# Third layer's attentions: two of four heads turned by VectorE and DMA instead of TensorE

## Chip, cores, metric

One of the cores of one Trainium2 chip. The time is device microseconds of a whole run of the program, which computes four layers one after another; lower is better.

## The reference

Four cross-attention layers follow each other on x (8, 256, 512). The change lies in the third one, which has a self attention, a cross attention and an MLP. Its attentions are, cut to what matters:

```python
NH = 16; HD = 32
def attention(q, k, v, mask):
    scores = jnp.einsum('bhqd,bhkd->bhqk', q, k) / jnp.sqrt(jnp.float32(HD))
    scores = scores * mask - 10000.0 * (1.0 - mask)
    probs = jax.nn.softmax(scores, axis=-1)
    return jnp.einsum('bhqk,bhkd->bhqd', probs, v)
ln_out = layernorm(hidden_states, ln1_s, ln1_b)
q, k, v = jnp.split(ln_out @ w_qkv + b_qkv, 3, axis=-1)
x = hidden_states + merge_heads(attention(..., ltor_mask)) @ w_ao + b_ao
q = layernorm(x, ln2_s, ln2_b) @ w_q + b_q
k, v = jnp.split(encoder_states @ w_kv + b_kv, 2, axis=-1)
x = x + merge_heads(attention(..., cross_mask)) @ w_co + b_co
```

Here hidden_states and encoder_states are (8, 256, 512): 8 batch elements, 256 rows, 16 heads of 32.

## The kernel before

`program` calls `l0_attention`, `l1_layer`, `l2_attentions` and `l2_mlp` in turn. `l2_attentions` goes through 16 **slots**: the self attention of the 8 batch elements (slots 0 to 7), then the cross attention of the 8 (slots 8 to 15). A slot has four **steps** (off 0 to 3), and a step k handles four heads ("quad"), so there are K = 64 steps. The order of the work on each engine is written out by hand in a loop over k; engines meet at semaphores. PSUM banks 0 to 3 hold the scores of the four heads, banks 4 to 7 are a ring: each label in `ring` takes the next of the four and waits until the one four before it is drained.

In step k each engine does, in this order:

- TensorE: `turn_probs(k-1, i)` for four heads (four 128x128 transposes each, L2297), the first half of a product for a neighbour slot (k, v and q for the next slot in off 0, 1, 2, the output projection p of the last slot in off 3; 24 matmuls of 256 columns or 12 of 512 in three passes hi/lo, L2363 and L2367), `turn_sums(k-1)` (L2306), `scores(k+1)` (L2286), `weigh_values(k-1)` (probabilities times values, L2321), then the second half of the product and, where a slot needs it, the turning of normalised x or of u (`turn_in`, L2384): in off 3 for self slots, in off 1 (x) and off 3 (u) for cross slots.
- ScalarE: `probs(k-1, i)` copies the turned probabilities of each head out of PSUM (L2421), `exponentials(k, i)` (L2414), the bias of k or q, copies of sums and outputs, the high half of what was turned in (T_hi), the store of x3.
- VectorE: the normalised rows xn (L931), `maxima(k, i)` (L2530, two per head), `low_outputs(k-2)` (L2548), the first half of v or p (L2565, L2568), `mask(k+1)` (scores out of PSUM times the mask, L2523, one per head), `outputs(k-1)` (values' sum times the reciprocal, L2543), T_lo (the low half of what was turned in, L2589, before which the next product can't start), the statistics of a row (L912), `reciprocals(k)`, the second half of v or p.
- GpSimd: the sums' reciprocals copied to rows, the standard deviations, the bias added to x (L2270).
- SP: all loads of the stage, each behind the wait it needs. It stands outside the loop over k.

The masked scores lie in `sc`, three of them in rotation; the probabilities are written in place, and turned into `probT`, two in rotation.

The first layer (`l0_attention`) turns its probabilities in another way: ScalarE writes them in runs of 32 (L566), VectorE transposes blocks of 32x32 (STREAM_TRANSPOSE, L797), and `move` (L281) brings the blocks to their partitions by 16 DMAs per half, issued by SP and GpSimd; its value matmuls read the result in runs of 32 elements.

## Time and profile before

| | |
|---|---|
| time, median of 3 runs | 3328.47 us (3325.46 to 3334.11) |
| profiled execution | 3319.85 us |
| its span | 3317.2 us |
| granted TensorE clock, mean | 0.963 |
| busy: PE, PEld, DVE, ACT, POOL | 93%, 72%, 71%, 53%, 21% |
| third layer's attentions | about 2130 to 2866 us of the span |

In the rows of a trace, PE is TensorE, DVE VectorE, ACT ScalarE, POOL GpSimd, SPq, ACTq and POOLq the queues that issue DMAs. Names like l2a_bank<-l2a_T_hi,l2a_w_hi_q are output and inputs by the program's names; L2363 is a line of the kernel. A bracket at the end of a row of a timeline is the idle time before it and who ended it.

### The profile page before, as it was taken

To read this page: it belongs to the slowest core of one execution; us is meant where nothing else is said; L and a number is where in the kernel's file an instruction comes from. 1 tells how busy PE (TensorE), PEld (TensorE's weight loads), DVE (VectorE), ACT (ScalarE), POOL (GpSimd) and SP (SyncE) were. 2 spreads that over 40 slices of the span, in tenths; PEclk is the share of its full clock that TensorE was granted. 3 is DMA by queue.
4 is the path that set the end of the run, shared out by engine and by line. 5 is a ranking of instruction groups with operands and counts; after the bars stand their busy time and mean duration, and the time that the engine had idled before them with its cause. 6 is when DMAs were issued, how large, how long until landed. Compare 5 with 4: busy or idle time off the path is not lost. (4 is left out here: it accounts for less than half of the span.)

```text
span 3317.2 us, 55559 instructions
## 1 busy us (share of the span) xinstructions
PE 3087.4 (93%) x20384; PEld 2377.3 (72%) x20384; DVE 2357.7 (71%) x3589; ACT 1742.7 (53%) x4185; POOL 698.2 (21%) x1206
## 2 busy tenths in 40 slices
PE   7999999999999977899999996689999999799999
PEld 6778788878878845566666663478887788587777
DVE  5777767777667656999999998167777878642321
ACT  4555445545454534465555643257787777532222
POOL 2554544545444430000000000011101111000000
PEclk9999999999999988899999998789999999899999
DMA  7779776877676664454455543300011111211000
GB/s 250 235 236 283 237 208 193 244 228 214 204 222 198 191 212 109 109 121 112 111 119 114 116 107 81 121 1 14 27 62 55 46 46 43 100 71 39 32 15 18
DMA packets 175325, 426.40 MB, mean 129 GB/s; under 512 B 52656, under 2 KB 60848, under 8 KB 150608
## 3 DMA queue, kind: packets, MB, share of 16 engines
q1 hardware_dynamic: 115936, 232.42, 25.3%
q10 hardware_dynamic: 28272, 127.46, 10.8%
q0 software_dynamic: 30848, 62.97, 7.6%
q8 instruction: 164, 2.69, 0.3%
q14 instruction: 105, 0.86, 0.1%
HBM read 229.76 MB, written 58.72 MB: 87 GB/s over the span
## 5 line engine op out<-in xcount | busy, mean ns | idle before, releaser
L281 POOL DMA_DIRECT2D l_probT<-l_prob x896 | 441.4, 500 | 253.7 <-DVE l_prob L797 234.3
L775 DVE TENSOR_REDUCE l_nmax<-l_bank 128x1 f32<-128x512 f32 x512 | 316.6, 680 | 182.3 <-PE l_bank L443 182.2
L566 ACT ACTIVATE l_prob<-l_bank,l_nmax 128x512 f32<-128x512 f32 x512 | 344.9, 689 | 132.8 <-DVE l_nmax L775 123.9
L797 DVE STREAM_TRANSPOSE l_prob<-l_prob 128x1024 f32<-128x1024 f32 x256 | 314.1, 1228 | 23.2 <-ACT l_prob L566 9.7
L409 PE MATMUL l_bank<-l_x_hi,l_w_hi 128*128 128x256 f32 x1024 | 298.3, 291 | 21.7 <-DVE l_x_lo L866 11.6
L409 PE MATMUL l_bank<-l_x_hi,l_w_lo 128*128 128x256 f32 x1024 | 291.4, 285 | 0.0
L409 PE MATMUL l_bank<-l_x_lo,l_w_hi 128*128 128x256 f32 x1024 | 291.0, 284 | 0.0
L1836 DVE TENSOR_TENSOR_SCAN l_kv<-l_wx,l_kv 128x2056 f32<-128x2056 f32 x64 | 283.8, 4434 | 3.1 <-DVE l_sxc L1957 1.5
L2414 ACT ACTIVATE l2a_sc<-l2a_sc,l2a_nmax 128x256 f32<-128x256 f32 x512 | 254.7, 508 | 41.0 <-DVE l2a_nmax L2530 41.0
L468 PE MATMUL l_bank<-l_probT,l_v 128*64 128x256 f32 x2048 | 241.4, 388 | 12.7 <-issue 6.8
L409 PEld LDWEIGHTS l_bank<-l_x_hi,l_w_hi 128*128 128x128 f32 x1024 | 197.6, 193 | 45.3 <-issue 37.4
L468 PEld LDWEIGHTS l_bank<-l_probT,l_v 128*64 128x64 f32 x2048 | 143.6, 139 | 104.8 <-issue 32.9
L2530 DVE CUSTOM_DVE_ANT_0 l2a_sc<-l2a_sc,l2a_mb 128x256 f32<-128x256 f32 x512 | 217.0, 483 | 0.0
L409 PEld LDWEIGHTS l_bank<-l_x_hi,l_w_lo 128*128 128x128 f32 x1024 | 198.0, 193 | 0.0
L409 PEld LDWEIGHTS l_bank<-l_x_lo,l_w_hi 128*128 128x128 f32 x1024 | 197.9, 193 | 0.0
L2523 DVE SCALAR_TENSOR_TENSOR l2a_sc<-l2a_bank,l2a_m 128x512 f32<-128x512 f32 x256 | 158.6, 680 | 54.2 <-PE l2a_bank L2286 54.2
L3069 DVE TENSOR_TENSOR l2b_h_lo<-l2b_hf,l2b_h_hi 128x512 fp32r<-128x512 f32 x64 | 44.2, 691 | 198.5 <-ACT l2b_h_hi L2975 198.3
L370 POOL TENSOR_TENSOR l_oT<-l_oT,l_rT 128x512 f32<-128x512 f32 x64 | 96.5, 1507 | 367.7 <-ACT l_oT L602 367.7
L1828 DVE TENSOR_TENSOR l_kv<-l_vb,l_ik 128x2048 f32<-128x2048 f32 x64 | 145.8, 2278 | 7.5 <-DMA l_vb<-vd 7.1
L427 PE MATMUL l_bank<-l_wv_hi,l_x_hi 128*128 128x256 f32 x512 | 148.3, 290 | 2.1 <-DVE l_wv_lo L834 2.1
L2297 PE MATMUL l2a_bank<-l2a_ident,l2a_sc 128*128 128x128 f32 x1024 | 133.2, 277 | 16.6 <-DVE l2a_oT L2543 8.7
L1844 DVE TENSOR_TENSOR l_kv<-l_kv,l_ir 128x2048 f32<-128x2048 f32 x64 | 146.1, 2284 | 0.1
(360 smaller groups left out, 7890.0 us busy)
## 6 DMA issues: line engine op xcount, KB each, us to landing
l_probT<-l_prob SPq DMA_DIRECT2D x1152, 64.0 KB, 2.9
l_vb<-vd SPq DMA_DIRECT2D x64, 1024.0 KB
l_probT<-l_prob POOLq DMA_DIRECT2D x896, 64.0 KB, 2.5
l_w_hi<-kept_w_hi ACTq DMA_DIRECT2D x24, 1024.0 KB, 5.7
l_w_lo<-kept_w_lo ACTq DMA_DIRECT2D x24, 1024.0 KB, 5.7
l_wv_hi<-kept_wv_hi ACTq DMA_DIRECT2D x12, 1024.0 KB, 8.3
l_wv_lo<-kept_wv_lo ACTq DMA_DIRECT2D x12, 1024.0 KB, 10.2
l2a_x<-x SPq DMA_DIRECT2D x16, 512.0 KB, 3.6
```

Source lines behind the costliest of these rows:

```text
L281: eng.dma_start(probT[i % RING][r * SQ:(r + 1) * SQ, g, :, :, :, :], prob[i % RING][g * SQ:(g + 1) * SQ, r * IT:(r + 1) * IT, :, :, :]).th ...
L409: mm = pe.matmul(s.ap[:, c * ROWS:(c + 1) * ROWS], a[:, kt, c, g, :], b[:, kt, c * ROWS:(c + 1) * ROWS], start=m == 0, stop=m == 3 * KT - 1)
L427: mm = pe.matmul(s.ap[:, at], a[:, kt, jt * P:(jt + 1) * P], b[:, kt, c, :, :], start=m == 0, stop=m == 3 * KT - 1)
L468: mm = pe.matmul(s.ap[own, f * ROWS:(f + 1) * ROWS], v[l][:, pair % 2, j, own], half[:, :, :, j, h, :], start=j == 0, stop=j == IT - 1)
L566: act.activation(prob[i % RING][:, :, it % 2, h, :].rearrange("p (q t) s -> p t q s", q=Q), s.ap[:, :].rearrange("p (t q s) -> p t q s", t ...
L775: dve.tensor_reduce(nmax[:, n % 2, it, h:h + 1], s.ap[:, :], AX.X, ALU.max, negate=True).then_inc(max_ready, 1)
L797: dve.transpose(own, own).then_inc(turned, 1)
L1836: dve.tensor_tensor_scan(own, wx[:, :, :].rearrange("p j t -> p (j t)"), own, 0.0, ALU.mult, ALU.add)\
L1844: dve.tensor_tensor(own, own, ir[:, ct, :].unsqueeze(1).to_broadcast([P, NJ, ROWS]), ALU.mult).then_inc(z_ready, 1)
L2414: ins = act.activation(to[:, r, :], to[:, r, :], ACT.Exp, scale=-1.0, bias=nmax[:, k % SC_RING, i, r:r + 1], accum_out=rsum[:, k % SC_RING ...
L2523: dve.scalar_tensor_tensor(out=sc[k % SC_RING][i][:, :, :], in0=s.ap[:, :].rearrange("p (r j) -> p r j", r=RT), scalar=HD ** -0.5, in1=own ...
L2530: dve.tensor_tensor_reduce(out=to[:, r, :], in0=to[:, r, :], in1=own[:, r, :], scale=-1.0, scalar=3.0e38, op0=ALU.add, op1=ALU.min, accum_ ...
```

## The change

Heads 0 and 1 of each quad no longer pass through TensorE. ScalarE writes their probabilities to a new buffer `prob` in runs of 32; `turn_blocks(k)` on VectorE transposes it in blocks of 32x32 (128x1024 elements) back into the place in `sc`; `move_heads(k)` moves the blocks to their partitions by 16 DMAs of 32 partitions x 256 elements (32 KB), 8 issued by SP and 8 by GpSimd, into `turned_by_dma` (two in rotation). `weigh_values` waits for them (`heads_moved`), and so does `mask` three steps later. Heads 2 and 3 go on as before. The ring has 2 labels fewer a step. On VectorE `turn_blocks(k)` stands before the masks of k+1, and `outputs(k-1)` stands between the masks of heads 0 and 1 and those of heads 2 and 3. On ScalarE `exponentials(k, 1)` comes ahead of the first half of the product. On GpSimd the moves stand after the bias and ahead of the deviations. On SP the loads are now taken in the loop over k, each behind the moves of its step.

```diff
--- before.py
+++ after.py
@@ -2036,7 +2036,7 @@
     return plan
 
 
-def l2_attentions(nc, kept_rows, rows_in, d, x2, u, mask_self, mask_cross, x3):
+def l2_attentions(nc, kept, kept_rows, rows_in, d, x2, u, mask_self, mask_cross, x3):
 
     SLOTS = [(b, a) for a in range(2) for b in range(B)]
     NS = len(SLOTS)
@@ -2046,6 +2046,10 @@
     XB = 4
     Q4 = range(QUAD)
     SC_RING, V_RING = 3, 2
+    BY_DMA, BY_PE = range(2), range(2, QUAD)
+    SQ, Q = 32, 4
+    MOVES = [(g, q) for g in range(Q) for q in range(Q)]
+    BY_SP = 8
     WEIGHTS = ["k0", "v0", "q0", "o0", "k1", "v1", "q1", "o1"]
     SPLIT_AT = {-5: "k0", -4: "v0", -3: "q0", -2: "o0", 25: "k1", 27: "v1", 28: "q1", 37: "o1"}
     NORMED = {"k0": 0, "v0": 0, "q0": 0, "q1": 1}
@@ -2092,7 +2096,7 @@
     ring = []
     for k in range(FIRST, LAST):
         quad = 0 <= k - 1 < K
-        ring += [f"t{k - 1}_{i}" for i in Q4] if quad else []
+        ring += [f"t{k - 1}_{i}" for i in BY_PE] if quad else []
         ring += ["b" + BIAS_AT[k]] if k in BIAS_AT else []
         what, z = product_of(k)
         ring += [f"{what}{z}_0"] if what else []
@@ -2123,10 +2127,18 @@
         scs = [ph.sb(f"sc{n}", [P, QUAD, RT, ROWS]) for n in range(SC_RING)]
         sc = [[s[:, i, :, :] for i in Q4] for s in scs]
         raw_sc = [s[:, :, :, :].rearrange("p i r n -> p (i r n)").rearrange("p (c n) -> p c n", c=CT) for s in scs]
-        probT = [[ph.sb(f"probT{n}{i}", [P, RT, ROWS]) for i in Q4] for n in range(2)]
+        probT = [{i: ph.sb(f"probT{n}{i}", [P, RT, ROWS]) for i in BY_PE} for n in range(2)]
+        turned_by_dma = [ph.sb(f"turned{n}", [P, Q, 2, RT, RT, SQ]) for n in range(2)]
+        blocks = [s[:, 0:2, :, :].rearrange("p i r n -> p (i r n)") for s in scs]
+        by_quarter = [a.rearrange("p (q e) -> p q e", q=Q) for a in blocks]
+        prob = ph.sb("prob", [P, Q * 2 * 2 * RT * SQ])
+        by_head = prob[:, :].rearrange("p (q i m s) -> p i m q s", q=Q, i=2, m=2 * RT)
         oT = [ph.sb(f"oT{i}", [P, ROWS]) for i in range(2)]
         oT_hi, oT_lo = [[ph.sb(f"oT_{part_}{i}", [P, CT, ROWS], F32R) for i in range(2)] for part_ in ("hi", "lo")]
         m, mb = [[ph.sb(f"{name}{i}", [P, RT, ROWS]) for i in range(2)] for name in ("m", "mb")]
+        turned_blocks = ph.sem("turned_blocks")
+        moved_sp = [ph.sem(f"moved_sp{n}") for n in range(2)]
+        moved_pool = [kept.enter_context(nc.semaphore(f"kept_moved_heads{n}")) for n in range(2)]
         nmax, rsum = ph.sb("nmax", [P, SC_RING, QUAD, RT]), ph.sb("rsum", [P, SC_RING, QUAD, RT])
         rinv = ph.sb("rinv", [P, 2, QUAD, RT])
         rows = ph.sb("rows", [P, RT, QUAD, HD])
@@ -2160,6 +2172,20 @@
         def drained(eng, s):
 
             eng.wait_ge(s.drained, s.k + 1)
+
+        def heads_moved(eng, k):
+
+            eng.wait_ge(moved_sp[k % 2], 16 * BY_SP * (k // 2 + 1))
+            eng.wait_ge(moved_pool[k % 2], 16 * (len(MOVES) - BY_SP) * (k // 2 + 1))
+
+        def move_heads(eng, k, pieces, moved):
+
+            eng.wait_ge(turned_blocks, k + 1)
+            if k >= 2:
+                full(eng, S[f"o{k - 2}"])
+            for g, q in pieces:
+                eng.dma_start(turned_by_dma[k % 2][q * SQ:(q + 1) * SQ, g, :, :, :, :].rearrange("p i r t s -> p (i r t s)"),
+                              by_quarter[k % SC_RING][g * SQ:(g + 1) * SQ, q, :]).then_inc(moved[k % 2], 16)
 
         def norm_count(z):
 
@@ -2227,20 +2253,17 @@
                     load_b(n)
                 load_m(0)
                 load_w("k1", "k0")
-                for z in range(4, B):
-                    load_x(z)
-                load_u(B)
-                load_x(B)
-                load_w("v1", "k1")
-                load_w("q1", "v1")
-                load_x(B + 1)
-                load_u(B + 1)
-                load_w("o1", "q1")
-                load_m(1)
-                for b in range(2, B):
-                    load_x(B + b)
-                    load_u(B + b)
-                    load_m(b)
+                for k in range(K):
+                    move_heads(sp, k, MOVES[:BY_SP], moved_sp)
+                    s, off = k // GROUPS, k % GROUPS
+                    if off == 0 and XB <= s + 2 < NS:
+                        load_x(s + 2)
+                    if k == 4 * B - 9 or off == 1 and B < s + 2 < NS:
+                        load_u(B if s + 2 < B else s + 2)
+                    if off == 3 and 0 < s - 6 < B:
+                        load_m(s - 6)
+                    if k in (25, 27, 29):
+                        load_w({25: "v1", 27: "q1", 29: "o1"}[k], {25: "k1", 27: "v1", 29: "q1"}[k])
                 sp.wait_ge(w_lo_ready, len(WEIGHTS))
                 for l in range(LANES):
                     sp.wait_ge(stored[l], 16 * (B // XB + 1))
@@ -2260,8 +2283,6 @@
                         pool.tensor_copy(rows[:, :, :, :], rinv[:, (k - 1) % 2, :, :].rearrange("p i r -> p r i").unsqueeze(3)
                                          .to_broadcast([P, RT, QUAD, HD])).then_inc(rows_ready, 1)
                     what, z = norm_of(k)
-                    if what == "stats":
-                        deviations(pool, mv, sd, eps, power, norm_count(z) - 1, 0, var_signal, sd_ready)
                     if what == "rows":
                         a = SLOTS[z][1]
                         pool.wait_ge(xn_ready, norm_count(z))
@@ -2269,6 +2290,10 @@
                         to = x[z % XB]
                         pool.tensor_tensor(to[:, :, :], to[:, :, :], brow[f"o{a}"][:, :].unsqueeze(1).to_broadcast([P, RT, COLS]),
                                            ALU.add).then_inc(xb_ready, 1)
+                    if 0 <= k < K:
+                        move_heads(pool, k, MOVES[BY_SP:], moved_pool)
+                    if what == "stats":
+                        deviations(pool, mv, sd, eps, power, norm_count(z) - 1, 0, var_signal, sd_ready)
 
             @block.tensor
             def _(pe):
@@ -2313,13 +2338,18 @@
                     if g == 0:
                         for half in range(2):
                             drained(pe, S[f"v{z}_{half}"])
-                    for i in Q4:
+                    for i in BY_PE:
                         drained(pe, S[f"t{k}_{i}"])
+                    heads_moved(pe, k)
                     for j in range(RT):
                         for i in Q4:
                             h = g * QUAD + i
+                            if i in BY_PE:
+                                prob = probT[k % 2][i][:, j, :]
+                            else:
+                                prob = turned_by_dma[k % 2][:, :, i, :, j, :].rearrange("p g r s -> p r g s")
                             mm = pe.matmul(s.ap[HD * i:HD * i + HD, 0:ROWS], v[z % V_RING][:, j, h * HD:(h + 1) * HD],
-                                           probT[k % 2][i][:, j, :], start=j == 0, stop=j == RT - 1)
+                                           prob, start=j == 0, stop=j == RT - 1)
                     mm.then_inc(s.full, 1)
 
                 def bias(n):
@@ -2387,7 +2417,7 @@
                 pe.wait_ge(consts, 2)
                 for k in range(FIRST, LAST):
                     if 0 <= k - 1 < K:
-                        for i in Q4:
+                        for i in BY_PE:
                             turn_probs(k - 1, i)
                     if k in BIAS_AT:
                         bias(BIAS_AT[k])
@@ -2409,9 +2439,13 @@
             def _(act):
                 def exponentials(k, i):
                     act.wait_ge(max_ready, RT * (k * QUAD + i + 1))
-                    to = sc[k % SC_RING][i]
+                    if i == 0 and k:
+                        act.wait_ge(turned_blocks, k)
                     for r in range(RT):
-                        ins = act.activation(to[:, r, :], to[:, r, :], ACT.Exp, scale=-1.0, bias=nmax[:, k % SC_RING, i, r:r + 1],
+                        own = to = sc[k % SC_RING][i][:, r, :]
+                        if i in BY_DMA:
+                            own, to = own.rearrange("p (t q s) -> p t q s", t=RT, q=Q), by_head[:, i, RT * r:RT * r + RT, :, :]
+                        ins = act.activation(to, own, ACT.Exp, scale=-1.0, bias=nmax[:, k % SC_RING, i, r:r + 1],
                                              accum_out=rsum[:, k % SC_RING, i, r:r + 1])
                     ins.then_inc(exp_ready, 1)
 
@@ -2486,15 +2520,15 @@
                 act.wait_ge(vec_in, 16)
                 for k in range(FIRST, LAST + 2):
                     if 0 <= k - 1 < K:
-                        for i in Q4:
+                        for i in BY_PE:
                             probs(k - 1, i)
                     if 0 <= k < K:
                         exponentials(k, 0)
+                        exponentials(k, 1)
                     product(k, 0)
                     if 0 <= k - 1 < K:
                         sums(k - 1)
                     if 0 <= k < K:
-                        exponentials(k, 1)
                         exponentials(k, 2)
                     if not turned_last(k):
                         turned(k)
@@ -2513,11 +2547,13 @@
 
             @block.vector
             def _(dve):
-                def mask(k):
+                def mask(k, heads):
                     own = m[mask_of(*SLOTS[k // GROUPS])]
                     if k == 0:
                         dve.wait_ge(w_lo_ready, WEIGHTS.index("o0") + 1)
-                    for i in Q4:
+                    if k >= SC_RING and heads == BY_DMA:
+                        heads_moved(dve, k - SC_RING)
+                    for i in heads:
                         s = S[f"s{k}_{i}"]
                         full(dve, s)
                         dve.scalar_tensor_tensor(out=sc[k % SC_RING][i][:, :, :], in0=s.ap[:, :].rearrange("p (r j) -> p r j", r=RT),
@@ -2529,6 +2565,10 @@
                     for r in range(RT):
                         dve.tensor_tensor_reduce(out=to[:, r, :], in0=to[:, r, :], in1=own[:, r, :], scale=-1.0, scalar=3.0e38,
                                                  op0=ALU.add, op1=ALU.min, accum_out=nmax[:, k % SC_RING, i, r:r + 1]).then_inc(max_ready, 1)
+
+                def turn_blocks(k):
+                    dve.wait_ge(exp_ready, QUAD * k + len(BY_DMA))
+                    dve.transpose(blocks[k % SC_RING], prob[:, :]).then_inc(turned_blocks, 1)
 
                 def reciprocals(k):
                     dve.wait_ge(exp_ready, QUAD * (k + 1))
@@ -2634,12 +2674,16 @@
                         bias(BIAS_AT[k])
                     if not (0 <= k < K and product_of(k)[0] == "p"):
                         product(k, 0)
+                    if 0 <= k < K:
+                        turn_blocks(k)
                     if 0 <= k + 1 < K:
                         if (k + 1) % GROUPS == 0 and SLOTS[(k + 1) // GROUPS][1] == 1:
                             dve.wait_ge(mb2_ready, SLOTS[(k + 1) // GROUPS][0] + 1)
-                        mask(k + 1)
+                        mask(k + 1, BY_DMA)
                     if 0 <= k - 1 < K:
                         outputs(k - 1)
+                    if 0 <= k + 1 < K:
+                        mask(k + 1, BY_PE)
                     if turned_last(k):
                         product(k, 1)
                     turned(k)
@@ -3167,7 +3211,7 @@
         between_layers.close()
         kept_rows = kept.enter_context(nc.sbuf_tensor("kept_rows", [P, CT, COLS], F32))
         rows_in = [kept.enter_context(nc.semaphore(f"kept_rows_in{l}")) for l in range(LANES)]
-        l2_attentions(nc, kept_rows, rows_in, d, x2, u, d["mask_self"], d["mask_cross"], x3)
+        l2_attentions(nc, kept, kept_rows, rows_in, d, x2, u, d["mask_self"], d["mask_cross"], x3)
         l2_mlp(nc, kept_rows, rows_in, d, x3, u, out)
 
 
```

## Rows read from the trace of the kernel before

**Rows 1.** Stretches: span, busy us (instructions) of five engines, clock, DMA share, GB/s; self and cross slot.

```profile
2290.00:2331.35 41.35, 40.90 (x355) 33.30 (x354) 32.63 (x105) 31.35 (x98) 5.05 (x7) 1.00 0.07 27
2638.20:2680.80 42.60, 41.70 (x362) 34.14 (x361) 34.12 (x109) 32.23 (x101) 5.16 (x7) 1.00 0.13 44
```

**Rows 2.** Timeline of SP's queue (start, us until the last ends, what, count): loads of x.

```profile
2283.31 124.39 SPq L2191 DMA_DIRECT2D l2a_x<-x  x4
```

**Rows 3.** Timeline of VectorE in a cross slot (start, us, what, count, idle before).

```profile
2624.42 1.06 DVE L931 TENSOR_SCALAR l2a_xn<-l2a_x,l2a_mv,l2a_sd 128x512 f32<-128x512 f32 x2 [1.01 <-POOL l2a_sd L925]
...
2635.07 1.29 DVE L2589 TENSOR_TENSOR l2a_T_lo<-l2a_bank,l2a_T_hi 128x512 fp32r<-128x512 f32 x2 [0.37 <-ACT l2a_T_hi L2468]
...
2649.82 0.69 DVE L2568 TENSOR_TENSOR l2a_x<-l2a_bank,l2a_x 128x512 f32<-128x512 f32 x1 [3.82 <-PE l2a_bank L2367]
...
2661.63 2.48 DVE L2523 SCALAR_TENSOR_TENSOR l2a_sc<-l2a_bank,l2a_m 128x512 f32<-128x512 f32 x4 [1.73 <-PE l2a_bank L2286]
...
2667.02 1.05 DVE L931 TENSOR_SCALAR l2a_xn<-l2a_x,l2a_mv,l2a_sd 128x512 f32<-128x512 f32 x2 [1.01 <-POOL l2a_sd L925]
```

**Rows 4.** Timeline of TensorE in the same cross slot: end of the wait for T_lo, q0, transposes.

```profile
2635.81 1.25 PE L2297 MATMUL l2a_bank<-l2a_ident,l2a_sc 128*128 128x128 f32 x8 [0.41 <-DVE l2a_T_lo L2589]
2636.82 0.36 PE L2363 MATMUL l2a_bank<-l2a_T_hi,l2a_w_hi_q 128*128 128x256 f32 x1
...
2644.97 1.91 PE L2297 MATMUL l2a_bank<-l2a_ident,l2a_sc 128*128 128x128 f32 x16
2646.63 0.51 PE L2367 MATMUL l2a_bank<-l2a_w_hi_o,l2a_oT_hi 128*128 128x512 f32 x1
```

**Rows 5.** Timeline of VectorE and TensorE in a self slot: T_lo, k0, v0, v1, masks.

```profile
2310.93 1.27 DVE L2589 TENSOR_TENSOR l2a_T_lo<-l2a_bank,l2a_T_hi 128x512 fp32r<-128x512 f32 x2
...
2313.33 0.36 PE L2363 MATMUL l2a_bank<-l2a_T_hi,l2a_w_hi_k 128*128 128x256 f32 x1
...
2326.29 0.69 DVE L2565 TENSOR_TENSOR l2a_v<-l2a_bank,l2a_b_v 128x512 f32<-128x512 f32 x1 [2.39 <-PE l2a_bank L2367]
...
2331.44 0.69 DVE L2565 TENSOR_TENSOR l2a_v<-l2a_bank,l2a_b_v 128x512 f32<-128x512 f32 x1 [1.05 <-PE l2a_bank L2367]
...
2337.20 2.48 DVE L2523 SCALAR_TENSOR_TENSOR l2a_sc<-l2a_bank,l2a_m 128x512 f32<-128x512 f32 x4 [1.97 <-PE l2a_bank L2286]
```

**Rows 6.** Groups by line, 2200 to 2490: the transposes on TensorE (busy us, mean ns, idle before).

```profile
L2297 PE MATMUL l2a_bank<-l2a_ident,l2a_sc 128*128 128x128 f32 x448 | 58.0, 279 | 6.7 <-DVE l2a_oT L2543 5.3 <-ACT l2a_rT L2428 1.4
```

**Rows 7.** First layer: transpose (ns min/median/max), one step's moves (timeline), landing (page, part 6).

```profile
L797 DVE STREAM_TRANSPOSE l_prob<-l_prob x256: 1187/1236/1247, 35.6 to 1196.4; 128x1024 f32<-128x1024 f32 x128
...
601.19 5.87 SPq L281 DMA_DIRECT2D l_probT<-l_prob  x9
...
601.46 3.46 POOL L281 DMA_DIRECT2D l_probT<-l_prob  x7 [0.73 <-DVE l_prob L797]
...
l_probT<-l_prob SPq DMA_DIRECT2D x1152, 64.0 KB, 2.9
```

**Rows 8.** Stretches with a gap on TensorE, and one stretch after it (columns as in rows 1).

```profile
390.00:393.00 3.00, 0.39 (x2) 0.00 (x0) 1.75 (x3) 0.00 (x0) 0.00 (x0) 1.00 1.06 242
393.00:397.00 4.00, 3.29 (x18) 2.17 (x20) 1.72 (x3) 2.79 (x8) 0.00 (x0) 0.57 0.85 245
...
1491.00:1494.00 3.00, 0.88 (x4) 0.48 (x3) 2.35 (x3) 3.00 (x5) 0.00 (x0) 1.00 0.53 131
...
2221.00:2226.00 5.00, 1.22 (x10) 0.74 (x7) 5.00 (x19) 4.48 (x16) 0.20 (x1) 1.00 0.00 0
2226.00:2233.00 7.00, 6.32 (x31) 6.32 (x32) 5.18 (x22) 4.34 (x13) 0.49 (x1) 0.52 0.00 0
```

**Rows 9.** Timeline of VectorE in the last slot: masks two steps apart, the last outputs.

```profile
2829.13 2.47 DVE L2523 SCALAR_TENSOR_TENSOR l2a_sc<-l2a_bank,l2a_m 128x512 f32<-128x512 f32 x4
...
2842.08 2.47 DVE L2523 SCALAR_TENSOR_TENSOR l2a_sc<-l2a_bank,l2a_m 128x512 f32<-128x512 f32 x4
...
2857.04 0.42 DVE L2543 TENSOR_TENSOR l2a_oT<-l2a_bank,l2a_rT 128x256 f32<-128x256 f32 x1 [2.75 <-PE l2a_bank L2321]
```

## The prediction

> **What bounds the kernel now.** I read the busy time of each engine in stretches first. In the third layer's attentions TensorE is busy for 40.9 of the 41.35 us that one slot of four steps takes in the self half, and 41.7 of 42.6 in the cross half; VectorE is at 32.6 and 34.1 [rows 1]. The pitch of a slot is read twice: four loads of x in 124.39 us, so 41.34 each [rows 2], and two normalisations 42.60 apart in the cross half [rows 3]. So TensorE sets the pace, but VectorE has only 8.5 us of idle per slot, and the timelines show where both meet. Two places matter. In cross slots VectorE ends T_lo (the low half of the turned x, off 1) at 2636.3; TensorE starts q0 at 2636.82, and VectorE gets p0 of the slot before at 2649.82, after 3.82 us of waiting [rows 3, 4]. In self slots T_lo (off 3) ends at 2312.2, TensorE starts k0 at 2313.33, and VectorE gets v0 at 2326.29 and v1 at 2331.44 [rows 5]. These chains across both engines decide what becomes of a lighter TensorE.
>
> **TensorE loses 8 transposes a step.** 16 take 1.91 us from the first start to the last end, 1.66 from their start to that of the product behind them (2644.97 to 2646.63) [rows 4], so two heads cost 0.83 us a step and 3.3 us a slot. The 448 transposes between 2200 and 2490 were 58.0 us busy [rows 6], so they are no small part. ScalarE loses two copies a step; it is not late anywhere in these rows, and I take nothing for it. The value matmuls now read runs of 32 elements and ScalarE writes such runs: the first layer does both all the time; I price both at nothing (a gain is impossible, and if each of the 8 reads took 0.05 us longer, 1.6 us a slot would go into TensorE's slack).
>
> **VectorE gains a transpose of 128x1024 a step.** The same instruction in the first layer takes 1236 ns [rows 7]; from one to the next it is about 1.2, which I take: 4.8 us a slot. By busy time alone the self slot would be VectorE's 32.6 + 4.8 + 1.0 (the wait for the deviations, 1.01 [rows 3]) = 38.4, the cross slot about 40.2. TensorE would be at 37.6 and 38.4. Both engines are then within 2 us of each other, so the chains decide.
>
> **Cross slots.** Chain on TensorE from T_lo's end to p0: 13.0 us now (2636.82 to 2649.82), less 0.83 for one group of two heads, plus 0.1 to start: 12.3. On VectorE from p0 to the next T_lo's end: the pitch 42.60 makes that end 2678.9, so 29.1 us, less the waits for TensorE and ScalarE in it, 1.73 and 0.37 [rows 3], is 27.0. The transposes of off 3, 0 and 1 lie in it and nothing there can hide them, since VectorE runs in order: + 3.6 = 30.6. Sum 42.9, less the 0.1 by which the rows overlap: 42.8, against 42.6 now. The 3.3 us off TensorE are thus not gained: only one of its four groups lies on this chain. 8 such slots (7 to 14): +0.2 each, **+1.6 us**.
>
> **Self slots.** TensorE from T_lo to v0: 12.96 now (2313.33 to 2326.29), less 0.83, plus 0.1: 12.2. From v0 to v1 TensorE needs 5.15 as now; VectorE would need 4.8. From v1 to the next T_lo's end VectorE takes 22.0 now (2331.44 to 2312.2 + 41.34), less 1.97 of waiting [rows 5], plus two transposes: 22.5. Sum 39.9: a gain of 1.5 a slot. Six slots (1 to 6): **-9.0 us**. Slot 0 has no projection, and VectorE waits in it; I take 0.
>
> **The DMAs.** Each step issues 8 on SP and 8 on the Pool queue. In the first layer 9 take SP 5.87 us and 7 take Pool 3.46 [rows 7], so SP needs 5.2 for 8 and Pool 4.0; an issue lands 2.9 us later [rows 7]. Together about 7.5 us from the transpose's end (pieces here have half the bytes, so rather less). I walked each slot with this: the transpose's end lies 8.3 us or more ahead of the value matmuls that need it, so some 0.8 us remain in self slots and 1.4 in cross slots. Cost: nothing, while this cover holds; every us beyond it is a us of TensorE on the chain. On SP, loads now queue behind the moves, and the moves of the next step behind a load that waits for a store: the store goes out at the end of step off 0, the next moves some 5 us later. On Pool the deviations come behind 4.0 us of issues; the statistics end about 4.3 us after the transpose, so sd is about as late as now. The rows copy has more time than that.
>
> **The outputs between the masks.** VectorE scales outputs(k-1) 1.2 us earlier. Now TensorE waits 0.4 to 0.5 us a slot for a bank it frees, and the ring has 6 labels a step in place of 8; no gain is left where VectorE sets the pace. The price of the new order is that masks 2 and 3 stand behind the value matmuls, 1.1 us after the first scores; the masks of heads 0 and 1 (1.2 us) cover it.
>
> **The clock.** With the chains above, TensorE in a cross slot ends the transposes of off 1 and then waits for T_lo: its work since the last chain point ends 3.7 us before. In the trace of before, such gaps are followed by a granted clock of half (1.2 instead of 2.4 GHz): after 2.6 of 3 us idle from 390 and after 3.8 of 5 from 2221, where the next 7 us ran at 0.52 [rows 8]. Of 18 gaps of more than 2.5 us that began at full clock between 60 and 2230 (those are the first and the last), 17 were followed by a fall; a gap of 2.12 (from 1491) was not [rows 8], and those near 2 us went either way. Four us at a mean of 0.57 (from 393) are 3.4 at half [rows 8]; so a fall costs 1.7 us of TensorE's work. In cross slots it falls on q0, on the chain: 8 x 1.7 = **+13.6**. In self slots the idle is 0.65 and 2.3 us with 0.85 of work between; I take a fall in half of six slots: **+5.1**. Bounds: 0 (the gaps don't lower it) and 3.4 a slot (a fall of 7 us, as after 2226).
>
> **The last slot and the end.** Slot 15 has no products but p; a step takes 6.5 us now (2829.13 to 2842.08 for two) [rows 9]. Two steps of the new loop are: moves 7.5, value matmuls and outputs 1.7, masks, maxima, transpose 5.7: 14.9, so 7.4 a step: 4 x 0.9 = **+3.6**. At the end the last value matmuls now end at 2857.0 [rows 9]; in the new kernel they wait for the last moves. The last transpose ends at about 2852.7, + 7.5 + 1.1 = 2861.3: **+4.3**, and the gap before it (4 us) makes the last projection run at half clock: **+1.7**.
>
> **Sum.** -9.0 + 1.6 + 13.6 + 5.1 + 3.6 + 4.3 + 1.7 = +20.9 us. The profiled execution took 3319.85 us (span 3317.2), so it would be 3340.8; the median of the runs is 8.6 us above it, so 3328.5 + 20.9 = **3349.4**. A measurement of this kernel can tell about 0.3% (10 us) from no change.
>
> A page of the Trainium skill speaks for the change: "VectorE: DVE Perf Modes", section "The three transpose paths", gives a 128x128 block of bf16 390 ns on TensorE and 311 on VectorE. The rows here (fp32, in streams) have 0.104 us a block on TensorE and 0.15 on VectorE, so the measured order is the reverse; by the page's ratio the transposes would cost VectorE 0.66 us a step and the cross chain would be 1.6 us shorter.
>
> **Rivals.**
> 1. *The clock holds.* Same chains, no falls: -9.0 + 1.6 + 3.6 + 4.3 = +0.5, **3329.0**. For it: gaps near 2 us went either way. Against: 17 of 18 above 2.5.
> 2. *The waits fill.* If the engines run further ahead of each other than my walk lets them, only busy time counts: self 38.4 (-3.0 x 6), cross 40.2 (-2.4 x 8), end +7.9: -29.3, **3299**. For it: VectorE waits 3.82 for p0 and TensorE never waits long now. Against: p0 stands in VectorE's order before the transposes that it would have to run ahead of.
> 3. *The moves are late* (slower still, and what decides against the change even without the clock). If they take 10 us from the transpose, 2.5 more than above, TensorE stands 1.7 longer in self and 1.1 in cross slots, twice in self: 6 x 3.4 + 8 x 1.1 = +29 beyond the forecast, **3378**. It starts to count from 8.3 us. For it: SP issues at 0.65 each, and one move is late if any is. Against: pieces are half as big, and the DMA share is 0.07 to 0.13 here [rows 1]. The skill's "SBUF — State Buffer", section "SBUF: two separate sides", says that Pool can't write descriptors while VectorE holds the shared port in a fast mode; by it xn (1.06 us) could hold Pool up by that much once a slot. The first layer's Pool issues [rows 7] show none.
>
> **Chances.** Forecast 0.44, clock holds 0.22, waits fill 0.24, moves late 0.10. Faster than 0.3%: the third and a little of the second, 0.26. Within: most of the second, a little of the first, 0.22. Slower: 0.52. The range that keeps 8 in 10 goes from 3298 (half of the fill case is left out) to 3372; the forecast's own is 3335 to 3362, its clock term between 0 and twice.
>
> **What would show it.** VectorE at 38 to 40 us busy a slot, with a wait for p0 of about 3 us left in cross slots; a cross pitch of 42.8 without falls and 44.5 with; a self pitch of 39.9 to 41.6; TensorE waiting for T_lo 2 to 4 us a slot; the granted clock under 1.00 in windows of cross slots; the value matmuls hardly waiting for the moves. Wrong if the cross pitch is under 42 (chain), if the clock stays 1.00 with gaps over 2.5 us, or if the value matmuls wait for a DMA for more than 1 us.

## Result and the profile after

The changed kernel takes 3335.8 us (median, 3329.4 to 3347.1), beside 3327.2 for the kernel before on the same chips: ratio 1.0028, 95% interval 1.0018 to 1.0037. So it is 9 us slower where 20.9 were forecast: the direction holds, the size is less than half. The interval lies clear of 1, but the loss is no larger than the 10 us that the prediction took as the least that can be told. The profiled execution took 3333.0 us (span 3331.2).

The page of the changed kernel, busy time and the DMAs (part 1, two lines of part 5 and two of part 6):

```profile
PE 3056.0 (92%) x19872; PEld 2338.6 (70%) x19872; DVE 2430.5 (73%) x3653; ACT 1681.4 (50%) x4057; POOL 951.5 (29%) x1718
...
L2187 POOL DMA_DIRECT2D l2a_turned<-l2a_sc x512 | 251.8, 499 | 317.4 <-DVE l2a_sc L2571 286.5
...
L2559 DVE SCALAR_TENSOR_TENSOR l2a_sc<-l2a_bank,l2a_m 128x512 f32<-128x512 f32 x256 | 161.4, 668 | 18.1 <-DMA l2a_turned<-l2a_sc 13.0
...
l2a_turned<-l2a_sc SPq DMA_DIRECT2D x512, 32.0 KB, 2.0
l2a_turned<-l2a_sc POOLq DMA_DIRECT2D x512, 32.0 KB, 1.8
```

A move takes GpSimd 0.50 us to issue and lands 1.8 to 2.0 us later. The 13.0 us for which the masks (L2559) seem to wait for a move are really waits for late scores: they come right after a fall of the clock (at 2635.50, say, 0.1 us after the scores end, when the move in question had long landed), and in e1, without the falls, they are gone from the cross slots. By the ends of T_lo on VectorE (one in each self slot, in off 3; two in each cross slot, in off 3 and off 1) the stage falls into stretches. All times are us from one profiled execution each:

| stretch | before | after | difference |
|---|---|---|---|
| six self slots (2187.6 to 2436.0 before) | 248.4 | 242.1 | -6.3 |
| change from self to cross (to 2507.5) | 71.5 | 65.3 | -6.2 |
| seven cross slots (to 2806.7) | 299.3 | 306.9 | +7.6 |
| last T_lo to last p | 57.7 | 70.2 | +12.6 |
| stage, first T_lo to the next stage's first instruction | 730.1 | 738.0 | +7.9 |

The expectations below still have 306.3, 70.8 and 13.2 for the changed kernel; they take the end of its last T_lo 0.6 us too early.

The rest of the profiled difference (3.8 ahead of the stage, 2.3 behind it) lies in code that is the same. The stretches answer to [rows 1]: one self slot, one cross slot with a fall of the clock, the change between the halves, the stretch with five cross slots, and the part of it right after a T_lo (columns as there):

```profile
2313.43:2353.20 39.77, 37.70 (x321) 29.80 (x320) 37.27 (x110) 27.25 (x90) 20.65 (x40) 1.00 0.29 81
2690.00:2734.00 44.00, 40.19 (x330) 32.34 (x329) 38.42 (x113) 28.51 (x92) 20.84 (x39) 0.96 0.31 91
2433.60:2498.90 65.30, 63.23 (x517) 51.65 (x516) 61.92 (x171) 47.52 (x143) 31.52 (x58) 0.95 0.40 123
...
2590.00:2810.00 220.00, 201.14 (x1640) 161.14 (x1639) 195.88 (x577) 144.57 (x468) 104.23 (x195) 0.96 0.30 87
2629.40:2632.80 3.40, 3.26 (x15) 3.29 (x16) 3.40 (x19) 2.22 (x9) 0.48 (x1) 0.50 0.62 180
```

In the self slot VectorE is busy for 37.3 us beside TensorE's 37.7: both ran up to the same level, as the sum had it (38.4 and 37.6), and a slot still takes 2.1 us more than either. The cross slot's clock is 0.96. VectorE's timeline where a cross slot turns x answers to [rows 3] (start, us, what, count, idle before):

```profile
2623.67 1.23 DVE L2571 STREAM_TRANSPOSE l2a_sc<-l2a_prob 128x1024 f32<-128x1024 f32 x1
...
2626.00 0.40 DVE L2583 TENSOR_TENSOR l2a_oT<-l2a_bank,l2a_rT 128x256 f32<-128x256 f32 x1
...
2627.53 0.67 DVE L2605 TENSOR_TENSOR l2a_v<-l2a_bank,l2a_b_v 128x512 f32<-128x512 f32 x1
2628.13 1.26 DVE L2629 TENSOR_TENSOR l2a_T_lo<-l2a_bank,l2a_T_hi 128x512 fp32r<-128x512 f32 x2
...
2643.20 0.69 DVE L2608 TENSOR_TENSOR l2a_x<-l2a_bank,l2a_x 128x512 f32<-128x512 f32 x1 [2.92 <-PE l2a_bank L2397]
```

The transpose (1.23 us) stands ahead of the scaled outputs, v1 and T_lo, and VectorE still waits 2.92 us for p0 (3.82 before). TensorE beside it, to compare with [rows 4]:

```profile
2623.89 1.06 PE L2414 MATMUL l2a_bank<-l2a_ident,l2a_xn 128*128 128x128 f32 x8
2626.46 0.66 PE L2322 MATMUL l2a_bank<-l2a_ident,l2a_sc 128*128 128x128 f32 x4 [1.50 <-DVE l2a_oT L2583]
2628.25 0.66 PE L2322 MATMUL l2a_bank<-l2a_ident,l2a_sc 128*128 128x128 f32 x4 [1.14 <-DVE l2a_v L2605]
2629.54 0.55 PE L2393 MATMUL l2a_bank<-l2a_T_hi,l2a_w_hi_q 128*128 128x256 f32 x1 [0.63 <-DVE l2a_T_lo L2629]
...
2633.93 0.27 PE L2331 MATMUL l2a_bank<-l2a_ident,l2a_rows 128*128 128x128 f32 x1
```

It waits 1.50, 1.14 and 0.63 us within 5 us, each time for the next thing that VectorE finishes, and then runs q0 at a granted clock of half for 3.4 us. In a self slot (compare [rows 5]) only the last wait is as long, and 3 us of a product lie between the second and the third:

```profile
2346.49 0.66 PE L2414 MATMUL l2a_bank<-l2a_ident,l2a_xn 128*128 128x128 f32 x4 [0.26 <-DVE l2a_x L2608]
2347.57 0.50 PE L2397 MATMUL l2a_bank<-l2a_w_hi_o,l2a_oT_hi 128*128 128x512 f32 x1 [0.42 <-ACT l2a_rT L2462]
2350.87 0.66 PE L2322 MATMUL l2a_bank<-l2a_ident,l2a_sc 128*128 128x128 f32 x4 [0.22 <-DVE l2a_oT L2583]
2352.66 0.66 PE L2322 MATMUL l2a_bank<-l2a_ident,l2a_sc 128*128 128x128 f32 x4 [1.14 <-DVE l2a_T_lo L2629]
```

TensorE in the last slot (compare [rows 9]): in the same view of before it waits 0.16 us once for the rows of the reciprocals; it now waits 2.5 to 4.4, then for the last moves, and scores and last projection start at half the clock.

```profile
2828.11 0.41 PE L2331 MATMUL l2a_bank<-l2a_ident,l2a_rows 128*128 128x128 f32 x2 [2.47 <-POOL l2a_rows L2283]
...
2835.88 0.66 PE L2331 MATMUL l2a_bank<-l2a_ident,l2a_rows 128*128 128x128 f32 x2 [3.39 <-POOL l2a_rows L2283]
2836.47 2.09 PE L2311 MATMUL l2a_bank<-l2a_k,l2a_q 32*128 32x256 f32 x16
...
2846.22 0.66 PE L2331 MATMUL l2a_bank<-l2a_ident,l2a_rows 128*128 128x128 f32 x2 [4.37 <-POOL l2a_rows L2283]
...
2863.50 0.41 PE L2331 MATMUL l2a_bank<-l2a_ident,l2a_rows 128*128 128x128 f32 x2 [3.57 <-POOL l2a_rows L2283]
2865.24 0.64 PE L2351 MATMUL l2a_bank<-l2a_turned,l2a_v 128*32 128x256 f32 x2 [1.33 <-DMA l2a_turned<-l2a_sc]
...
2868.72 0.76 PE L2397 MATMUL l2a_bank<-l2a_w_hi_o,l2a_oT_hi 128*128 128x512 f32 x1 [1.54 <-DVE l2a_oT_lo L2588]
```

### The profile page after: what moved, and what is told of

It is laid out like the page before. It is cut to its first block and busy times, and to the rows that moved or that the text cites. A ratio compares the mean times of both kernels' runs of the same rounds, so it can differ in the third digit from the quotient of the medians.

```text
span 3331.2 us, 55617 instructions
## 1 busy us (share of the span) xinstructions
PE 3056.0 (92%) x19872; PEld 2338.6 (70%) x19872; DVE 2430.5 (73%) x3653; ACT 1681.4 (50%) x4057; POOL 951.5 (29%) x1718
## 3 DMA queue, kind: packets, MB, share of 16 engines
q10 hardware_dynamic: 28272, 127.46, 10.8%
## 5 line engine op out<-in xcount | busy, mean ns | idle before, releaser
L2187 POOL DMA_DIRECT2D l2a_turned<-l2a_sc x512 | 251.8, 499 | 317.4 <-DVE l2a_sc L2571 286.5
L409 PE MATMUL l_bank<-l_x_hi,l_w_hi 128*128 128x256 f32 x1024 | 299.0, 292 | 20.8 <-DVE l_x_lo L866 11.3
L2559 DVE SCALAR_TENSOR_TENSOR l2a_sc<-l2a_bank,l2a_m 128x512 f32<-128x512 f32 x256 | 161.4, 668 | 18.1 <-DMA l2a_turned<-l2a_sc 13.0
L2448 ACT ACTIVATE l2a_prob<-l2a_sc,l2a_nmax 128x256 f32<-128x256 f32 x256 | 127.2, 503 | 79.6 <-DVE l2a_nmax L2566 79.1
```

The lines of the kernel that those rows point to most:

```text
L409: mm = pe.matmul(s.ap[:, c * ROWS:(c + 1) * ROWS], a[:, kt, c, g, :], b[:, kt, c * ROWS:(c + 1) * ROWS], start=m == 0, stop=m == 3 * KT - 1)
L2187: eng.dma_start(turned_by_dma[k % 2][q * SQ:(q + 1) * SQ, g, :, :, :, :].rearrange("p i r t s -> p (i r t s)"), by_quarter[k % SC_RING][g ...
L2559: dve.scalar_tensor_tensor(out=sc[k % SC_RING][i][:, :, :], in0=s.ap[:, :].rearrange("p (r j) -> p r j", r=RT), scalar=HD ** -0.5, in1=own ...
```

## Experiments

Every ratio is against the kernel before on the same chip, with its 95% interval; the changed kernel's is 1.0028. The stretches of each profile:

| kernel | self | change | cross | end | ratio |
|---|---|---|---|---|---|
| before | 248.4 | 71.5 | 299.3 | 57.7 | |
| changed | 242.1 | 65.3 | 306.9 | 70.2 | 1.0028 (1.0018 to 1.0037) |
| e1 TensorE kept busy in cross slots | 242.6 | 65.3 | 298.5 | 67.6 | 0.9999 (0.9987 to 1.0011) |
| e2 half of each transpose | 238.8 | 63.8 | 297.5 | 66.5 | 0.9974 (0.9960 to 0.9989) |
| e3 outputs after all masks | 243.4 | 68.7 | 310.0 | 70.7 | 1.0061 (1.0042 to 1.0081) |
| e4 more of ScalarE's time | 242.3 | 66.1 | 306.2 | 71.5 | 1.0036 (1.0022 to 1.0051) |
| e5 self slots only | 242.6 | 67.7 | 299.3 | 57.7 | 0.9975 (0.9960 to 0.9991) |
| e6 self slots and off 2 | 244.8 | 65.2 | 294.7 | 56.8 | 0.9956 (0.9940 to 0.9972) |
| e7 not in the last slot | 243.8 | 65.2 | 308.4 | 59.4 | 0.9999 (0.9985 to 1.0012) |
| e8 all moves on SP | 288.3 | 77.7 | 358.9 | 88.4 | 1.0388 (1.0363 to 1.0413) |
| e9 outputs' place alone | 248.5 | 70.9 | 295.4 | 59.0 | 0.9989 (0.9976 to 1.0002) |
| e10 off 2 and outputs' place | 244.6 | 65.3 | 290.7 | 56.7 | 0.9932 (0.9916 to 0.9947) |
| e11 ScalarE issues at the end | 244.3 | 66.2 | 307.0 | 75.4 | 1.0040 (1.0028 to 1.0052) |
| e12 no GpSimd moves at the end | 242.2 | 65.2 | 306.3 | 69.0 | 1.0027 (1.0015 to 1.0039) |
| e13 TensorE kept busy at the end | 242.6 | 66.0 | 306.3 | 73.1 | 1.0042 (1.0025 to 1.0060) |

A self stretch moves by up to 2.7 us from profile to profile of the same code there (242.1 to 244.8): in e6, e7, e10 and e11 the third self slot has a fall of the clock and takes 41.5 in place of 39.8. A cross stretch moves by 2 with the number of falls.

**e1: is it the clock?** In `turn_probs` and `turn_in`:

```diff
+                    for _ in range({2: 3, 3: 2}[i] if k >= 4 * B and k % GROUPS == 1 else 1):
+                        for _ in range(3 if what == "x" and z > B else 1):
```

> Added to the changed kernel: TensorE repeats transposes that it has just made, with the same data into the same banks, in the cross slots only: those of x three times (off 1), those of heads 2 and 3 at the start of off 2 three times and twice. They lie where TensorE waits for VectorE (1.50, 1.14 and 0.63 us in the slot that starts at 2607), so no chain gets longer. Theory (a gap of 3.3 us with 1.3 us of work in it makes the granted clock fall, and each fall costs 1.6 us of a slot): the falls after 2585 that stand at T_lo of off 1 (five of seven cross slots) go, every such slot takes about 42.4 us in place of 44.0, and the kernel gets 8 us faster (3328). Rival (the falls have another cause, or the filler itself delays ScalarE's copies and q0): the falls stay, or the pitch stays near 44 without them; the time is 3336 or above.

No fall is left between 2500 and 2820, each cross slot takes 42.5 us (19.7 + 22.8), and the stretch gave back 8.4 us where 8 were expected. The fall at the head of the last slot is gone too, and the end is 2.6 us shorter. TensorE where it waited before:

```profile
2631.11 1.09 PE L2323 MATMUL l2a_bank<-l2a_ident,l2a_sc 128*128 128x128 f32 x8 [0.24 <-DVE l2a_v L2607]
2632.40 0.36 PE L2394 MATMUL l2a_bank<-l2a_T_hi,l2a_w_hi_q 128*128 128x256 f32 x1 [0.20 <-DVE l2a_T_lo L2631]
```

The stretch with five cross slots (columns as in [rows 1]; the changed kernel's row is above, with 201.1 us busy and a clock of 0.96):

```profile
2590.00:2810.00 220.00, 215.53 (x1857) 175.13 (x1858) 202.79 (x586) 149.63 (x483) 107.65 (x202) 1.00 0.32 90
```

TensorE is busy for 215.5 of 220 us, 14 more than in the changed kernel, mostly with repeats that nobody needs, and the kernel is as fast as before. What had cost time was the idle time's effect on the clock, not the idle time.

**e2: VectorE's part of the chains.**

```diff
-                    dve.transpose(blocks[k % SC_RING], prob[:, :]).then_inc(turned_blocks, 1)
+                    dve.transpose(blocks[k % SC_RING][:, 0:512], prob[:, 0:512]).then_inc(turned_blocks, 1)
```

> The transpose on VectorE covers only the first 512 of its 1024 columns in each step; half of the turned blocks is left out, everything else runs as before. It takes about 0.65 us in place of 1.23. Theory (two chains across both engines set the pace; three of four transposes lie on the one of a cross slot, two on the one of a self slot): cross slots without a fall 42.4 - 1.8 = 40.6 us, self slots 39.8 - 1.2 = 38.6 us. Rival (VectorE's busy time alone is the bound): 2.4 us less in both, 40.0 and 37.4. Rival (the moves or TensorE are the bound): less than 0.5 in both. With shorter gaps some of the falls of the clock may go too, 1.6 us each. In all some 22 to 33 us faster by the chains (3303 to 3314).

```profile
L2571 DVE STREAM_TRANSPOSE l2a_sc<-l2a_prob 128x512 f32<-128x512 f32 x63 | 44.1, 699 | 0.0
```

A half transpose takes 0.70 us, so 0.53 is saved each, not 0.6. Cross slots without a fall took 41.2 (19.2 + 22.0), 1.3 less where three transposes on the chain would give 1.6. Self slots took 39.2, 0.6 less where two would give 1.1, hardly more than the 0.5 that the second rival allows. Busy time alone (four, 2.1) is excluded. Where time is missing, VectorE has a new wait for TensorE's scores: 0.52 us in a self slot (at 2334.98) and 0.65 in a cross slot without a fall (at 2755.79). In all the kernel is 18 us faster than the changed one, less than the 22 to 33 expected.

**e3: the outputs between the masks.**

```diff
                         mask(k + 1, BY_DMA)
+                        mask(k + 1, BY_PE)
                     if 0 <= k - 1 < K:
                         outputs(k - 1)
-                    if 0 <= k + 1 < K:
-                        mask(k + 1, BY_PE)
```

> Undoes one part: VectorE scales outputs(k-1) after all four masks again, all else as in the changed kernel. My prediction held this part for nothing. By the trace the scaling ends 1.2 us later, and TensorE waits 1.2 us longer for its bank at the start of off 2, but T_lo ends when it did: 0 us a slot from the chains. The longer gap (2.7 in place of 1.5) lets the clock fall in all seven cross slots in place of five: +3 us at most. Rival (the place of the outputs is what makes the change bearable, for instance through the low half of the outputs, or through the bank): 0.5 us or more a slot, 8 us or more in all.

11 us slower than the changed kernel: the rival holds. The profiles show 8.3 us of it in the stage: 3.1 in the seven cross slots, 3.4 in the change between the halves, 1.3 in the self slots (one has a fall) and 0.4 at the end. VectorE and TensorE at the turn of x:

```profile
2685.18 1.29 DVE L2629 TENSOR_TENSOR l2a_T_lo<-l2a_bank,l2a_T_hi 128x512 fp32r<-128x512 f32 x2 [0.38 <-ACT l2a_T_hi L2502]
```

```profile
2684.27 1.25 PE L2322 MATMUL l2a_bank<-l2a_ident,l2a_sc 128*128 128x128 f32 x8 [2.70 <-DVE l2a_oT L2583]
```

The scaled outputs come 1.2 us later; ScalarE rounds them (oT_hi) before it copies T_hi; so T_hi is late and T_lo waits 0.38 us, which it does not in the changed kernel. The interval off 3 to off 1 is 23.3 in place of 22.8 in each slot, the wait for the bank 2.70 in place of 1.50, and of the seven intervals from off 1 to off 3 now six have a fall of the clock, in place of five.

**e9: the same edit on the kernel before.** Its `mask(k + 1)` in two calls of two heads, `outputs(k - 1)` between them.

> One part alone: the kernel before, with outputs(k-1) scaled between the masks of heads 1 and 2 and nothing else of the change. My prediction held this for nothing; the version of the changed kernel without it was 11 us slower than the changed kernel, so it may be worth something here too. Theory (the place matters through ScalarE: its high half of the outputs stands ahead of its copies of T_hi, which VectorE waits 0.38 us for before T_lo in cross slots): cross slots get 0.4 us shorter, seven of them 299.3 to 296.5, and T_hi is no longer waited for; self slots change by less than 0.3; in all 3 to 5 us faster than before, 0.1%. Rival (it only pays beside the transposes on VectorE, which push the outputs later and open a gap in which the clock falls): less than 1 us in the seven slots.

The seven slots take 3.9 us less; a cross slot 42.2 in place of 42.6, and T_lo waits for T_hi no more. The kernel's ratio is 0.9989, whose interval just takes in 1. So this small part pays by itself in the cross slots, though its worth for the whole kernel is not clear of the noise; beside the transposes it is worth more (e3).

**e4: ScalarE.** Each copy of a turned head in four pieces of 128 columns.

> ScalarE copies each turned head (2 and 3) in four pieces of 128 columns in place of one of 512, which by about 0.2 us for each further instruction costs it 0.6 us more a head, 4.8 us a slot: as much as the change took from it. Theory A (the three slots around the change from self to cross, 71.5 us before and 65.3 after, were gained because ScalarE has the weights' splits there and was late): they go back to 68 us or more, while steady self and cross slots stay within 0.3 us. Theory B (TensorE's 24 fewer groups of transposes brought that gain): they stay within 1 us of 65.3. If ScalarE's copies stand on the steady chains against my forecast, the self slots get 0.5 us or more longer.

ScalarE gets busier by only 1.1 us a self slot (28.35 beside 27.25), a quarter of what was meant, since small copies cost less than I assumed (eight in 1.47 us). Steady slots don't move, the change gets 0.8 us longer. So 1.1 us more of ScalarE's time cost nothing in steady slots, and between A and B this run does not decide; the busy times speak for B (below).

**e5, e6, e7, e10: where the DMA path pays.** A predicate decides for each step; where it is false, TensorE turns all four heads into the same memory (`probT` laid over `turned_by_dma`), with the order of ScalarE and VectorE of the kernel before.

```diff
+    def by_dma(k):
+        return k < 4 * B                                             # e5
+        return k < 4 * B or k % GROUPS == 2 and k < K - GROUPS       # e6, e10
+        return k < K - GROUPS                                        # e7
```

> VectorE and the DMA queues turn heads 0 and 1 only in the self slots (steps 0 to 31); from step 32 on TensorE turns all four, in the order of work of the kernel before. Theory (self slots gain 1.6 us each by their chain, the change from self to cross gains by TensorE's load, cross slots lose by the clock, the last slot by the moves): self slots 39.8 as in the changed kernel, cross slots 42.6 to 44.0 for two intervals as before (306.3 us for the seven slots), no loss at the end; some -6.3 for the self slots, -3 to -6 for the change between halves, against the kernel before: 10 to 12 us faster than before, 0.3 to 0.4%. Rival (the self slots' gain is given back when TensorE meets its next limit, the transition): within 0.1% of before.

8 us faster than before (3319.8 beside 3327.4), a little less than the 10 to 12 expected: 5.8 in the self slots and 3.8 in the change. Cross slots and end are as before (299.3, 57.7).

> As the self-only version, and in cross slots also the one step (off 2) whose transpose on VectorE does not lie between p0 and the next T_lo, but whose two heads TensorE would turn between T_lo and p0. By my account of the cross chain (12.3 us on TensorE with one group less, VectorE's part as before, 29.1 less nothing) each cross slot takes 0.8 us less than before, seven slots 306.3 - 5.6 = 300.7; 16 us faster than before in all. Rival (transposes cost VectorE time wherever they stand, 1.2 us a slot): seven cross slots 306 or more.

The kernel is 16 us faster, as expected. A cross slot of it (columns as in [rows 1]):

```profile
2667.50:2709.30 41.80, 40.78 (x354) 33.21 (x353) 35.51 (x110) 31.15 (x98) 9.31 (x15) 1.00 0.19 58
```

From the second cross slot on a slot takes 41.8 us (18.9 + 22.9), 0.8 less than 42.6: the group of TensorE's transposes between T_lo and p0 is gone, and VectorE's transpose stands where VectorE had been waiting for p0 anyway. The third is 1 us longer, as it is in the kernel before, and the first gained nothing. So the stretch is 4.6 shorter, not 5.6. (The 300.7 of the forecast starts from 306 us, which was not the kernel before; from its 299.3 it would have been 293.7, and 294.7 was measured.)

> As the changed kernel up to step 59; in the last slot (steps 60 to 63) TensorE turns all four heads. Theory (the last slot lost 13.2 us: the copy of the reciprocals' rows stands behind 3.9 us of issues on GpSimd and TensorE waits for it 2.5 to 4.4 us a step, the last value matmuls wait for the last moves, and the clock is at half from 2834 on): the time from the last T_lo to the last p goes from 70.8 back to about 58, 13 us less than the changed kernel (3323 for a median of 3336). Rival (the loss there comes from VectorE's transposes alone, 4.8 us, or from something before the slot): 5 us less at most.

End 59.4; 9 to 10 us of the changed kernel's loss are gone (ratio 0.9999), 10.8 by the profile. The rival allowed 5.

> The version with VectorE's turning in the self slots and in off 2 of cross slots, with the outputs scaled between the masks in every step, also in those where TensorE turns all heads. If the effects add up, the cross slot goes from 41.8 to 41.4 and the kernel gets 3 us faster than the version without (3311 to 3308). Rival (the gain of the outputs' place stands on the same chain that is short now): the same within 1 us in the stage.

The effects add up: 41.4 us a cross slot, 3304.7 us beside 3328.1, 0.7% faster than before. A cross slot of it:

```profile
2632.00:2673.40 41.40, 40.64 (x355) 33.30 (x354) 35.48 (x110) 31.07 (x98) 9.31 (x16) 1.00 0.19 60
```

TensorE is busy for 40.6 of 41.4 us at full clock; this is the fastest version that was run.

**e8: how much cover do the moves have?** `BY_SP = 16`, none on GpSimd.

> All 16 moves of a step are issued by SP in place of 8 there and 8 on GpSimd. At 0.6 us an issue the last one lands 16 x 0.6 + 1.9 = 11.5 us after the transpose, against 6.8 now. Theory (cover of 8.3 us between a transpose and the value matmuls that need it): TensorE waits about 3 us a step for a DMA in most steps; part is on the chain: self slots 3 us or more longer, cross slots 2 or more, in all 30 us or more slower than the changed kernel. In the last slot the rows copy is free of the issues: if the copy's place behind them is what costs there, TensorE's waits for GpSimd (2.5 to 4.4 us a step) go. Rival (the cover is larger than I walked it): under 1 us a slot.

SP's queue and TensorE in a self slot:

```profile
2329.75 20.76 SPq L2207 DMA_DIRECT2D l2a_turned<-l2a_sc  x31
2350.56 0.59 SPq L2237 DMA_DIRECT2D l2a_x<-x  x1
```

```profile
2340.85 0.41 PE L2371 MATMUL l2a_bank<-l2a_turned,l2a_v 128*32 128x256 f32 x2 [3.27 <-DMA l2a_turned<-l2a_sc]
```

130 us slower than before and 120 slower than the changed kernel, four times what I expected: 8 us a self slot in place of 3. 31 issues take 20.8 us, so 64 take 43 us of a slot that lasted 40, and loads come on top: SP has become a bound of its own, beside the latency. The clock falls in self slots too (0.93 in the slot from 2282 to 2333). TensorE waits 58 times for a move, up to 6.6 us. That the cover can be used up is shown; that it ends at 8.3 us is not, since here the moves fall behind by more than the longer issue. In the last slot the waits for GpSimd are under 1 us, with 3.8 to 6.6 us for moves in their place.

**e11, e12, e13: the last slot.** e11: `move_heads(act, k, MOVES[BY_SP:], moved_act)` behind `exponentials(k, 3)` for the last four steps, in place of GpSimd's. e12: GpSimd's moves left out there. e13: `for _ in range(7 if k >= K - GROUPS and i == 3 else 1)` around the transposes of head 3.

> The changed kernel, but in the last slot (steps 60 to 63) ScalarE issues the eight moves that GpSimd issues elsewhere; VectorE's transposes, SP's moves and all counts stay. Theory (what the last slot lost is first the copy of the reciprocals' rows behind GpSimd's issues: waits of 2.47, 3.39, 4.37 and 3.57 us): TensorE's waits for GpSimd go, and from the last T_lo to the last p it takes 62 to 65 us in place of 70.8, since the moves themselves still have to land. Rival (the copy is late but the moves land no earlier, so that the wait only changes its name): 70 us, with waits for a DMA in the place of those for GpSimd.

```profile
2855.28 0.42 ACT L2484 ACTIVATE l2a_oT_hi<-l2a_oT 128x256 fp32r<-128x256 f32 x1 [4.42 <-issue]
```

Inconclusive, and slower (75.4): ScalarE loses 4.4 to 5.0 us a step to the issues and is late with everything else.

> The changed kernel, but in the last slot (steps 60 to 63) GpSimd's eight moves are left out with nothing in their place, so half of the turned blocks of these steps is stale; SP's eight, VectorE's transposes and the waits for SP's moves stay. SP's moves last longer (8 x 0.59 + 1.9 us) than GpSimd's (8 x 0.50 + 1.8), so the time of the last landing hardly changes. Theory (the issues on GpSimd hold up the copy of the reciprocals' rows, for which TensorE waits; giving them to ScalarE only held up ScalarE instead, by 4.4 to 5.0 us a step): from the last T_lo to the last p 63 to 66 us in place of 70.8, with waits for GpSimd under 1.5 us. Rival (the copy is late by the reciprocal, and the step is as long as VectorE's transpose and SP's moves make it): 69 us or more.

```profile
2836.22 0.66 PE L2331 MATMUL l2a_bank<-l2a_ident,l2a_rows 128*128 128x128 f32 x2 [2.14 <-POOL l2a_rows L2283]
2841.03 0.64 PE L2351 MATMUL l2a_bank<-l2a_turned,l2a_v 128*32 128x256 f32 x2 [2.13 <-DMA l2a_turned<-l2a_sc]
...
2863.66 0.64 PE L2351 MATMUL l2a_bank<-l2a_turned,l2a_v 128*32 128x256 f32 x2 [2.88 <-DMA l2a_turned<-l2a_sc]
```

The end takes 69.0, so the rival holds: only 1.2 us came back. Without GpSimd's issues much of the time is waited for SP's moves (2.13 and 2.88 us), and the first two waits for the rows stay (2.47, and 2.14 in place of 3.39).

> The changed kernel, and in the last slot (steps 60 to 63) TensorE makes the transposes of head 3 seven times in place of once (same data, same bank), 2.5 us of work in the 3.4 to 4.4 us that it waits there for GpSimd and the moves. Theory (a third of the 13.2 us lost between the last T_lo and the last p is the granted clock: scores at 2.09 in place of 1.15 us twice, value matmuls at 0.64 in place of 0.39 three times, the first third of the last product): the falls from 2834 on go, and the stretch takes 64 to 67 us in place of 70.8. Rival (VectorE and the moves set the step there, TensorE's slow work lies beside them or the filler delays ScalarE's copy of head 3): 69 us or more, even with the clock at 1.00.

```profile
2835.32 3.25 PE L2323 MATMUL l2a_bank<-l2a_ident,l2a_sc 128*128 128x128 f32 x28 [0.36 <-ACT l2a_sc L2449]
2839.35 0.41 PE L2332 MATMUL l2a_bank<-l2a_ident,l2a_rows 128*128 128x128 f32 x2 [0.78 <-POOL l2a_rows L2283]
2839.69 1.15 PE L2311 MATMUL l2a_bank<-l2a_k,l2a_q 32*128 32x256 f32 x16
```

The scores of step 61 are back at 1.15 us and TensorE waits 0.78 instead of 3.39, yet from one transpose of the rows to the next it is 7.78 us, as in the changed kernel (2828.11 to 2835.88: 7.77). In that step neither TensorE nor its clock sets the time; by VectorE's outputs the next step gains 0.6 (7.85 for 8.44). In the last two steps the filler itself stood ahead of the projection of the slot before, so the stretch got longer (73.1), and the clock's share there stays open.

## Why the prediction was right or wrong, point by point

By stretches, the forecast of +20.9 was -3.9 for the self slots (chain and clock), +1.9 for the change between the halves (the price of one cross slot), +13.3 for seven cross slots and +9.6 for the end. Measured were -6.3, -6.2, +7.6 and +12.6. The largest miss, 8.1 us, is the change between the halves; the next, 5.7, are the cross slots.

**Self chain: right.** 39.9 forecast, 39.8 measured in four of six slots. The stretch gained 6.3 and not 9.0, since the first two gained only 0.4 and 0.8, and one slot took 40.6 (a late start of GpSimd's issues, below). Where the first two meet, the clock was at half for 6.8 us before and is for 10.2 now, 1.7 us more of TensorE's work; that would account for most of the 1.8 that they lack, but no run tries it. That VectorE's two transposes lie wholly on this chain is not borne out: half of them gave 0.6 of 1.1 (e2).

**Clock in self slots: wrong, +5.1 did not come.** My walk put 2.3 us of idle into one gap; the trace has 1.14 at most, the rest is spread over three places with a product between, and no steady self slot shows a fall. The step that failed is the gap that the walk put into one piece. Falls are rare there rather than excluded: in e6, e7, e10 and e11 the third slot has one, after the same waits (0.28, 0.43, 0.23 and 1.14 us in e7), and loses 1.7. In e6 it follows T_lo:

```profile
2294.00:2297.40 3.40, 3.40 (x18) 3.40 (x17) 3.40 (x19) 2.17 (x9) 0.15 (x1) 0.50 0.18 45
```

**Cross chain: right, in part by luck.** 42.8 forecast, 42.5 without a fall. Undoing three quarters of it (e6) and halving VectorE's part (e2) move it in the forecast direction by 0.7 and 1.3. But the sum took off VectorE's wait of 0.37 for T_hi without saying what would end it. It is the place of the outputs that ends it: in e3 the wait is back, and off 3 to off 1 takes 23.3 in place of 22.8.

**Clock in cross slots: right in mechanism, smaller in sum.** 1.7 a fall forecast, 1.6 measured (21.3 for 19.7). I counted eight; six came, five within the seven slots (one of them cost 2.4), in all some 9 us, of which e1 took back 8.4, and the sixth at the head of the last slot, where it is counted with the end. The gap before a fall is in pieces here, 1.50, 1.14 and 0.63 us with 0.66 between, no longer one of 3.7, and two of seven slots got by. The waits alone do not tell which: 1.28, 1.14 and 0.63 before 2587.0 had no fall behind them, 1.26, 1.14 and 0.63 before 2717.5 had one. The rule for one long gap was also a little less sure than stated: the trace of before has 19 such gaps, and neither the one of 2.59 us from 1196.7 nor the one of 3.42 from 1206.9 was followed by a fall. In e3, with a first piece of 2.70, six of seven fell, all but the first after the change of halves.

**The change between the halves: missed, -6.2.** My sum priced self slots 1 to 6 and cross slots by their steady chains and left these two marks at the cross price. In the trace of before this stretch is TensorE's; the same view as [rows 1], and its transposes by line before and after:

```profile
2436.00:2507.50 71.50, 69.07 (x569) 57.22 (x568) 55.26 (x165) 53.94 (x156) 5.91 (x9) 0.95 0.17 61
...
L2297 PE MATMUL l2a_bank<-l2a_ident,l2a_sc 128*128 128x128 f32 x101 | 12.8, 274 | 0.2 <-DVE l2a_T_lo L2589 0.2
...
L2322 PE MATMUL l2a_bank<-l2a_ident,l2a_sc 128*128 128x128 f32 x49 | 6.9, 275 | 1.1 <-DVE l2a_v L2605 0.7 <-DVE l2a_T_lo L2629 0.4
```

TensorE is busy for 69.1 of 71.5 us there and VectorE for only 55.3, 16 us idle. TensorE's idle time stays (2.4 before, 2.1 after) and its busy time falls by 5.8 (69.07 to 63.23), nearly the whole gain; the transposes alone fall by 5.9. The step that failed is that I laid the steady chains over a stretch that has its own balance, without reading its row. TensorE's load is not all of it, though: with the outputs after the masks (e3) the stretch takes 68.7, so VectorE's order has to let the gain through.

**Outputs between the masks: wrong.** Held for nothing; worth 11 us beside the transposes (e3) and some 4 alone (e9, by the cross slots). The step that failed reads "no gain is left where VectorE sets the pace": I looked at the bank that VectorE frees, and not at ScalarE, whose next work in order (T_hi) VectorE waits for. The row was there: T_lo waits 0.37 us for T_hi in [rows 3].

**ScalarE's copies: right** for steady slots (e4). **The moves: right.** Value matmuls waited three times for a move, 1.9 us in all, of which 1.33 at the very end, where the sum had a wait. With the moves far later it is nearly every step (e8). Reading runs of 32 costs them nothing either: 396 ns a matmul, beside 397 for heads 2 and 3. That SP goes past what it can issue was not among my rivals, since 16 moves on it were not forecast.

**Last slot and end: too small, 9.6 for 12.6.** From one scaling of the outputs to the next it took 7.6 to 10.2 us, not 7.4. "The rows copy has more time than that" was wrong there, for GpSimd copies the rows only after 3.9 us of issues, but e12 gives it only 1.2 us. 10.8 of the 12.6 hang on the DMA path in this slot (e7); e7 keeps the other 1.8, and with them the fall at the slot's head. By e2 3.7 of it go with half of the transposes' time. How the rest divides between the moves' latency and the clock is not settled.

**Rivals.** "The clock holds" gives about the time of e1: the changed kernel without its falls is at 3326.9, where I said 3329.0. That is partly luck: beside that rival's own terms, e1 is 6.4 us better in the change between the halves and 2.2 in the cross slots, 3.2 worse in the self slots and 2.1 at the end. "The waits fill" is excluded (self slots 39.8, not 38.4). "The moves late" is excluded for this kernel. The forecast's terms -9.0, +1.6, +13.6, +5.1, +3.6, +4.3 and +1.7 became -6.3, about -1.5, +9, 0 and +12.6 for the last three, and -6.2 was not in it: +7.9 in the stage, with 0.2 at its edges.

## What to carry to other kernels

When work moves from the busiest engine to the second busiest, write down for each step whether its new place stands before or behind the point at which that engine waits anyway. Here the same transpose was free in off 2, while in off 3, 0 and 1 together it made a cross slot 1.1 us longer even without a fall of the clock (42.5 beside 41.4 in e10), and the version that used this was 0.7% faster than before. Ask of a freed TensorE also where its idle time will gather, because a gap can cost more by the clock than by itself; and follow a moved instruction to the engine that waits for it and on to that engine's next work.

## What the runs showed of the hardware

GpSimd's first issue of a step begins 0.3 us after VectorE's transpose, but once in 15 steps (120 issues) 3.2 us after it, with SP's on time: at 2358.2, 2514.6, 2677.9 and 2838.6 in the changed kernel. It is steps 16, 31, 46 and 61 in e1, e3 and e4 too, at other times, and 16 and 31 in e5, e6 and e10; step 46 of e6, whose moves are only the 36th set, starts on time. So it seems to go by the number of issues. SP's queue and GpSimd's in step 61:

```profile
2838.59 1.14 SPq L2187 DMA_DIRECT2D l2a_turned<-l2a_sc  x2
```

```profile
2831.43 3.91 POOL L2187 DMA_DIRECT2D l2a_turned<-l2a_sc  x8 [3.46 <-DVE l2a_sc L2571]
2835.33 0.41 POOL L2283 COPY l2a_rows<-l2a_rinv 128x256 f32<-128x256 f32 x1
2841.76 3.91 POOL L2187 DMA_DIRECT2D l2a_turned<-l2a_sc  x8 [6.03 <-issue]
```

The transpose of step 61 ended at 2838.56. A self slot of 39.8 us becomes 40.6 by it; in the last slot it falls on the step of 10.2 us, but e12 has no such hold there and gains only 1.2 us. What holds GpSimd then, the profile doesn't show, and no run tried it.

An fp32 transpose on VectorE was 1.23 us for 128x1024 and 0.70 for 128x512, so 0.17 are fixed and 32 columns take 0.033. A 128x128 block is then 0.154 us, and still needs the moves, beside 0.104 on TensorE [rows 4]. The Trainium skill ("VectorE: DVE Perf Modes", section "The three transpose paths") has it the other way round, 311 ns on VectorE and 390 on TensorE for a block of bf16; the trace disagrees for streams of fp32 blocks, and the measured order is the one that the cross chain paid.

The granted clock fell to half (1.2 of 2.4 GHz) after waits that were no longer one gap: 1.26 to 1.50, 1.14 and up to 0.63 us with two groups of transposes between, in five intervals of seven; in e1, with 0.24 and 0.20 left, in none.
